# A decoder layer on one core: the first two pairs of heads staged by halves of the tokens beside the projections, and later casts moved from VectorE to GpSimd

## The reference

```
x = layernorm(x + causal_attention(x))            # 16 heads of 16 features, rotary q and k
x = layernorm(x + cross_attention(x, ctx, mask))  # 77 context rows
x = layernorm(x + ffn(x))                         # 256 -> 1024 -> 1024 -> 1024 -> 256, silu gate, gelu, gelu
```

## Time and profile before

| | |
|---|---|
| median of 3 runs | 871.85 us (871.64 to 872.28) |
| the profiled execution's own time | 867.16 us |
| its span in the trace | 865.4 us |
| mean granted clock of TensorE | 0.974 of full speed |
| busy: PE, DVE, ACT, POOL | 803.2, 479.6, 376.2, 321.4 us |

### The profile page before, as it was taken

One profiled execution on the slowest core, in us unless ns is written; L12 is line 12 of the kernel. 1 busy time (PEld: TensorE's weight loads), 2 busy tenths in 40 slices (PEclk: granted clock), 3 DMA queues, 4 the chain that ended last, 5 costly groups with the idle time before them and its releaser, 6 DMA issues.

```text
span 865.4 us, 14094 instructions
## 1 busy us (share of the span) xinstructions
PE 803.2 (93%) x5044; PEld 542.1 (63%) x5044; DVE 479.6 (55%) x1257; ACT 376.2 (43%) x768; POOL 321.4 (37%) x585
## 2 busy tenths in 40 slices
PE   8879988898998999999999888989899899999996
PEld 4544444346776777877777634433577678887886
DVE  3797878536675542155444888871477661125113
ACT  0686776773444211223212377767544432113110
POOL 6313325245312543445332424323631143335433
PEclk9957999999999999999999999999999999999999
DMA  9900534430000232434332035510000000000000
GB/s 274 411 29 33 195 119 147 149 131 1 2 2 25 73 122 74 145 116 141 109 123 73 26 123 182 227 58 2 2 1 2 2 2 1 0 7 20 1 1 26
DMA packets 24712, 68.70 MB, mean 79 GB/s; under 512 B 4449, under 2 KB 11873, under 8 KB 24417
## 3 DMA queue, kind: packets, MB, share of 16 engines
q1 hardware_dynamic: 24640, 67.77, 22.4%
HBM read 65.40 MB, written 13.63 MB: 91 GB/s over the span
## 4 chain that ended last, share of the span: by engine, by line
PE 77%; DVE 10%; ACT 8%; issue 3%; POOL 2%; POOLq 0%; ACTq 0%; DVEq 0%
PE bank_pair L906 27%; PE bank_pair L729 7%; PE bank_pair L894 6%; PE bank_pair L711 6%; ACT prob_s L1048 5%; PE bank_pair L824 4%; PE bank_pair L615 3%; PE bank_pair L761 3%; PE bank_pair L675 3%; DVE bank_pair L1236 3%; PE bank_pair L659 3%; DVE max_raw L1234 3%; PE bank_pair L836 2%; PE bank_pair L903 2%; PE bank_pair L813 2%
## 5 line engine op out<-in xcount | busy, mean ns | idle before, releaser
L1539 POOL TENSOR_TENSOR hid_lo_s<-act_raw_s,hid_hi_s 128x512 fp32r<-128x512 f32 x96 | 124.5, 1298 | 175.4 <-DVE hid_hi_s L1383 136.4
L1048 ACT ACTIVATE prob_s<-bank_pair 128x512 f32<-128x512 f32 (+3 forms) x384 | 163.6, 505 | 57.0 <-PE bank_pair L711 56.5
L1236 DVE CUSTOM_DVE_ANT_0 bank_pair<-bank_pair,causal_bf 128x128 f32<-128x128 f32 (+3 forms) x256 | 120.2, 515 | 43.9 <-PE bank_pair L675 43.5
L675 PE MATMUL bank_pair<-k_t_s,q_t_s 64*128 64x512 f32 (+3 forms) x384 | 120.5, 439 | 3.2 <-DVE max_raw L1234 2.1
L711 PE MATMUL bank_pair<-q_t_s,k_t_s 64*128 64x512 f32 (+3 forms) x384 | 114.5, 409 | 8.4 <-ACT prob_s L1048 4.6
L1500 POOL TENSOR_SCALAR_AFFINE_SELECT prob_s<-prob_s 128x128 f32<-128x128 f32 x256 | 72.0, 295 | 132.1 <-ACT prob_s L1048 129.1
L1383 DVE CAST hid_hi_s<-act_raw_s 128x512 fp32r<-128x512 f32 x64 | 35.9, 565 | 144.8 <-ACT act_raw_s L1115 144.2
L1115 ACT ACTIVATE act_raw_s<-bank_pair,scales 128x512 f32<-128x512 f32 x64 | 42.9, 688 | 160.2 <-PE bank_pair L906 160.2
L711 PEld LDWEIGHTS bank_pair<-q_t_s,k_t_s 64*128 64x128 f32 x384 | 55.7, 190 | 90.5 <-ACT prob_s L1048 69.0
L906 PE MATMUL bank_pair<-hid_hi_s,home_s 128*128 128x512 f32 x256 | 99.8, 390 | 0.8 <-POOL hid_lo_s L1539 0.8
L906 PE MATMUL bank_pair<-hid_lo_s,home_s 128*128 128x512 f32 x256 | 99.6, 389 | 0.0
(11 more groups left out here) (157 smaller groups left out, 1422.3 us busy)
## 6 DMA issues: line engine op xcount, KB each, us to landing
ring_s<-scratch SPq DMA_DIRECT2D x34, 512.0 KB, 3.3
home_s<-scratch SPq DMA_DIRECT2D x22, 512.0 KB, 6.0
checked_s<-in_w_ffn SPq DMA_DIRECT2D x2, 3584.0 KB, 18.2
scratch<-in_w_ffn SPq DMA_DIRECT2D x2, 2560.0 KB, 10.1
ring_moved_s<-scratch SPq DMA_DIRECT2D x10, 512.0 KB, 3.3
checked_s<-in_w_ffn SPq DMA_DIRECT2D x1, 4096.0 KB, 32.4
x_t_s<-in_x_t SPq DMA_DIRECT2D x4, 512.0 KB, 4.2
x_tok_s<-in_x SPq DMA_DIRECT2D x2, 1024.0 KB, 9.1
```

The costliest lines, as they stand in the source:

```text
L675: mm(out[:, 0:k1 - k0], qkt(q, p, 0)[r, P * qt:P * (qt + 1)], qkt(q, p, 1)[r, k0:k1], start=True, stop=True).then_inc(S["max_mm"], 1)
L1048: act.activation(prob[q][4 * (s % 2) + j][:, 0:n], score_bank(s, j)[:, 0:n], ACT.Exp, scale=SCALE).then_inc(S["exp_done"], 1)
L1236: dve.tensor_tensor_reduce(out=out[:, 0:left], in0=out[:, 0:left], in1=L["causal_bf"][:, CHUNK - left:CHUNK], scale=1.0, scalar=NEG, op0=A ...
L1539: pt(dst[1][:, m], act_raw[q][r % 3][:], dst[0][:, m].bitcast(F32), ALU.subtract).then_inc(S["f_lo"], 1)
```

## The change

Sequence 0 alone: the staging, turning and units 0 to 7 of pairs 0 and 1 are done for the first half of the tokens beside the projections (at t = 4 to 11), and the second half of pair 0 is staged and turned there as well (t = 9, 12, 13); pair 1's second half is staged at t = 14. The steps before 0 that remain run from -11 instead of -20. In them run the two last turns of pair 1 (-11, -10), the 16 other units of pair 0 (-11 to -8) and of pair 1 (-7 to -4). The maxima of pair 0 are moved at step -7 instead of -9. The 22 checks of weights are put two to a step into steps -11 to -1. The first 16 units use two banks alternately.

In both sequences: for pairs 2 to 7 the two casts of `stage_hi` are done by GpSimd instead of VectorE, ahead of the two subtractions, which are GpSimd's before and after the change.

```diff
+FIRST_STEP = (-11, pair_base(0) - 13)
+Q_STEP = FIRST_STEP[0] - (NT + V_LAG[0])
+STAGES = [[(Q_STEP + 4, 0, 0), (Q_STEP + 7, 1, 0), (Q_STEP + 9, 0, 1), (Q_STEP + 14, 1, 1)] +
+          [(pair_base(p) - 13, p, None) for p in range(2, NP)], [(pair_base(p) - 13, p, None) for p in range(NP)]]
-def turn_step(p, i):
+def turn_step(q, p, i):
+    if q == 0 and p < 2:
+        return ((Q_STEP + 6, Q_STEP + 6, Q_STEP + 12, Q_STEP + 13), (Q_STEP + 9, Q_STEP + 9, -11, -10))[p][i]
     return pair_base(p) - 12 + i
-def max_step(p, u):
+def max_step(q, p, u):
+    if q == 0 and p < 2:
+        return Q_STEP + 7 + 3 * p + u // 4 if u < 8 else -11 + 4 * p + (u - 8) // 4
     return pair_base(p) - 8 + u // 4
 def check_step(n):
-    return FIRST_STEP + 4 + n * (-FIRST_STEP - 4) // PIECES
+    return FIRST_STEP[0] + n // 2
...
     def unit_bank(q, n):
+        if q == 0 and n < Q_UNITS:
+            return bank[n % 2]
...
         for t in range(NT + V_LAG[0]):
             projections(0, t)
+            attention(0, Q_STEP + t)
...
+        # VectorE: pairs 0 and 1 alone
+        def stage_hi(q, n):
+            step, p, half = STAGES[q][n]
+            t0, t1 = (0, NT) if half is None else (NT // 2 * half, NT // 2 * (half + 1))
...
+        # GpSimd: pairs 2 to 7
+        def stage_hi(q, n):
+            step, p, half = STAGES[q][n]
+            wait(pool, q, "round_mm", ROUND_AT[q][("turn", p - 1, 3)] + 1)
             for i in range(2):
+                src = qk_tok[q][:, i, p].rearrange("p t (h e) -> p (t h) e", h=2).unsqueeze(2).to_broadcast([P, 2 * NT, 2, DH])
+                pool.tensor_copy(stage[q][i][:, :, 0:3 if i else 2:2 if i else 1], src).then_inc(S["stage_hi"], 1)
...
         def attention(q, s):
-            for p in range(1, NP):
-                if stage_step(p) == s:
-                    stage_lo(q, p)
+            for n, (step, p, half) in enumerate(STAGES[q]):
+                if step == s and p >= 2:
+                    stage_hi(q, n)
+                if step == s and n:
+                    stage_lo(q, n)
             if 0 <= s < LAST:
                 select(q, s)
```

More of the change, by code:

```diff
@@ L119, with turns_done @@
 S_END = FINAL_STEP + 1
[L121 to L128, removed]
+ROUNDS = [[], []]
+for _q in range(BATCH):
+    for _s in range(Q_STEP, FINAL_STEP + 1):
+        ROUNDS[_q] += [("turn", p, i) for p in range(NP) for i in range(4) if turn_step(_q, p, i) == _s]
+        ROUNDS[_q] += [("rows", p, 0) for p in range(NP) if rows_step(_q, p) == _s]
+        ROUNDS[_q] += [("y", n, 0) for n in range(2 * NG) if y_step(n) == _s]
+        if _s == 0:
+            EARLY = len(ROUNDS[_q])
+ROUND_AT = [{r: n for n, r in enumerate(rounds)} for rounds in ROUNDS]
+assert ROUNDS[0][EARLY:] == ROUNDS[1][EARLY:]
+def turns_done(q, p, i):
+    return sum(r[0] == "turn" for r in ROUNDS[q][:ROUND_AT[q]["turn", p, i] + 1])
 XG = NG // 2
@@ L138 @@
 X_END = XG * (NT - 1) + X_NORM + 4
[L142 removed]
+LATE_SCORE = 4 * (1 + max(max_step(0, p, u) for p in range(NP) for u in range(NU)))
 BY_VECTOR = [4 * end > LATE_SCORE for end in CHUNK_END]
@@ L179 @@
 FLAG_BANK = 5
-FIRST_UNITS = (2 * NU, sum(max_step(p, u) < 0 for p in range(NP) for u in range(NU)))
+Q_UNITS = 16
+FIRST_UNITS = (2 * NU, sum(max_step(1, p, u) < 0 for p in range(NP) for u in range(NU)))
 SHARED = (6, 2)
@@ L480, in consumer @@
     def consumer(q, n):
-        kind = ROUNDS[n][0]
-        count = sum(r[0] == kind for r in ROUNDS[:n + 1])
+        kind = ROUNDS[q][n][0]
+        count = sum(r[0] == kind for r in ROUNDS[q][:n + 1])
         name = {"turn": "turn_evac", "rows": "rows_evac", "y": "y_norm"}[kind]
@@ L1157, in _ @@
             projections(0, t)
-        for s in range(FIRST_STEP, S_END):
+            attention(0, Q_STEP + t)
+        for s in range(FIRST_STEP[0], S_END):
             attention(0, s)
@@ L1451, in _ @@
         dve.wait_ge(set_pool, 11)
-        for t in range(NT):
-            projections(0, t)
-        for s in range(FIRST_STEP, S_END):
+        for t in range(NT + V_LAG[0]):
+            if t < NT:
+                projections(0, t)
+            attention(0, Q_STEP + t)
+        for s in range(FIRST_STEP[0], S_END):
             attention(0, s)
@@ L1600, in _ @@
         fill(0)
-        for t in range(NT + 1):
-            projections(0, t)
-        for s in range(FIRST_STEP, S_END):
+        for t in range(NT + V_LAG[0]):
+            if t <= NT:
+                projections(0, t)
+            attention(0, Q_STEP + t)
+        for s in range(FIRST_STEP[0], S_END):
             attention(0, s)
```

123 lines of the change are left out of this document (65 added, 58 removed).

## The result

The changed kernel takes 880.64 us (median of 6 runs, 878.02 to 883.44), the kernel before in the same session 871.75 us (866.42 to 873.35). The ratio is 1.0117, 95% interval 1.0086 to 1.0149: slower, by 8.9 us between the medians. The forecast was 876.5, in a range of 870.0 to 882.5. The profiled execution of the changed kernel took 883.35 us, span 881.6. That of the kernel before (867.16) was one of its shorter ones: of its 93 runs in the three later sessions 32 lie at 866 to 868 us and the others at 869 to 877. The two traces therefore stand 16 us apart, more than the kernels do.

The account below looks back on a forecast made before the run. The prediction took TensorE as the bound (busy 93%, 77% of the chain). Late checks, 3.5 us, plus GpSimd's casts, 1.2 us, gave 4.7 us more: the median of 871.85 becomes 876.5 us, range 870.0 to 882.5 (8 in 10).

Parts of the forecast that it names:

- the sum: Whole kernel: 3.5 us from late checks plus 1.2 us from GpSimd's casts, 4.7 us more.
- the second rival: Clock stays low through the projections, or casts cost near their upper bound: +7 to +13 us, chance 17%.
- the full forecast: Projections end at about 43 us, checks late, small cost on GpSimd: +2.5 to +7 us, chance 45%.
- Projections stretched: Opening: work moved beside the projections makes them end at 43.5 us instead of 31.75.
- The schedule at full clock: Projections followed step by step on TensorE without clock loss: last copy ends at 41.5 us, 9.8 us more.
- The lull: TensorE idles before the third unit, waiting for VectorE among the projections: some 2.5 us.
- my bound of 49.5: Latest end of the projections, with the low clock costing 8 us on all remaining tiles and turns.
- Checks behind the last v copy: Opening: ScalarE's 22 checks wait for the last v copy; first exponential 4.0 us later, costing 3.5 us.
- Casts on GpSimd: Stagings of pairs 2 to 7: 0.7 us a cast, 1.2 us in all, from 0 to 10 us.
- The delay of 0.3 us at steps 10 and 22: Masks queued behind GpSimd's staging make the turn wait 0.3 us, four times in two sequences: 1.2 us.
- The sign: Whole kernel: slower by over 0.2%, chance 0.66, resting on the checks coming late.
- No gain from VectorE's relief: VectorE loses 24 casts, 10 us of 480, but is not on the chain there: no gain counted.

Follow-up runs that it names:

- b3: Changed kernel with 24 idle transposes before the third unit and the 22 weight checks spread from step -18 on; ratio 1.0064 to the kernel before.
- a2: Changed kernel with all casts back on VectorE, so the change of the opening alone; ratio 1.0121 to the kernel before.
- a3: Changed kernel whose weight checks read 16 values of each row instead of 1024; ratio 1.0072 to the kernel before.
- b2: Changed kernel with the 22 weight checks spread from step -18 on instead of two a step from -11; ratio 1.0112 to the kernel before.
- b1: Changed kernel with 24 idle transposes, whose result nobody reads, put before the third unit; ratio 1.0054 to the kernel before.
- a1: Kernel before with the casts of pairs 2 to 7 on GpSimd and nothing else; ratio 1.0045 to the kernel before.

## Why the prediction was right, and where its sizes were off

The time lies in the range, but the sum is about half of what was measured: 4.7 us forecast, 8.9 measured. The measured value lies in the span of the second rival (+7 to +13, 17%) and not in that of the full forecast (+2.5 to +7, 45%); the range held because it reached into the rival's.

- **Projections stretched: right, too small.** Two terms were too small. The schedule at full clock was one: I had 17.1 us from the first unit (24.4) to the end of the last copy (41.5), where b3 shows 18.9 to the end of the last v tile and a copy takes 0.4 more. The lull was put at 2.5 us and was 2.89. The clock was the other: I took 2 us, between none and 4, with the end at 43.5. It was 2.5 us in a2, a3 and b2 and 7.0 in the profiled execution, where the clock was low for some 17 of the 23 us from 27 to 50. There the copy ended at 50.24, beyond even my bound of 49.5. That is the rival "clock stays low through the projections". The Trainium skill, "TensorE: Matmul & The Clock Gate", "HAM oscillation — how this bites in real kernels", describes matmuls that fall back to half rate behind a wait; here the trace agrees: the clock went from 1.00 to 0.50 behind a wait of 2.89 us.
- **Checks behind the last v copy: right.** I had 29.7 us from the last v copy's end to the first exponential; the trace has 29.9, and so have a2 (46.52 to 76.41) and b1 (44.73 to 74.62). ScalarE has no idle between the checks that matters, the chain names them, and TensorE waits 0.90 us for the first exponential before its fourth score. Their share of the loss, about 4 us by a3, can be taken away but wasn't won back by an earlier place. The first exponential itself came behind the 71 to 76 us that I had named (80.14, and 76.41 in a2), because the projections ended later than named.
- **Casts on GpSimd: price a little high, no wait seen.** 0.61 us against 0.7 assumed, just below my lower bound of 0.65. The Trainium skill, "GPSIMD Engine Reference", section 3.1, has 768 ns for 512 elements; this measurement is lower. The delay of 0.3 us at steps 10 and 22 didn't come: the casts lengthen a staging by 0.97 us and not by 1.3, and before the change the masks had ended 1.1 us ahead of the products. So no trace shows the 1.2 us of the sum. That the opening alone costs as much as the whole change says the same; a1 is the one number against it, and the ratios are too coarse to tell 1.2 us from nothing.
- **The sum.** 3.5 + 1.2 became 10.9 + 0 in the profiled pair, 7.2 + 0 with a2's opening, and 8.9 between medians. The sign and its mechanism were right.
- **No gain from VectorE's relief: right.** It lost 5.2 us of work, not 10: back to back, a cast holds the queue for 0.34 us (35.89 to 36.23 in the trace before) and not for 0.42, and two of the new half casts took 1.38 us. From the first exponential to the turn of step 22 it is 67.4 us before and 67.5 after.

## What to carry to other kernels

Work that is moved into another stage's queue costs what its waits do to everything behind it in that queue: here some 7.7 us of VectorE's work were hidden at the price of 15 to 18 us on an in-order TensorE (the last copy of v ends at 46.5 to 50.2 us instead of 31.75). Ask of a third engine, even one with no part in the moved work, whether its own load can still fit once its start moves: 28.5 us of ScalarE that had been hidden became the critical path. A lull in a dense stretch of TensorE is to be counted with what the clock does behind it: here 2.89 us of waiting were followed by 2.5 to 7 us lost at half the clock. Whether that costs anything depends on whether TensorE is the bound there. And one trace is one execution: the same opening had its first exponential at 76.41 in one trace and at 80.14 in another.

## What the runs showed of the hardware

- 24 additional transposes, 2.84 us of work in a wait, made the changed kernel 5.5 us faster (1.0117 to 1.0054); in the trace TensorE's granted clock stays at 1.00 for ten microseconds more. A similar filling in the kernel before, where VectorE and ScalarE are nearly full, changed nothing (1.0000).
- A GpSimd cast of 128x512 from float32 to fp32r with a repeated input took 0.61 us, VectorE's 0.42.
- In the changed kernel one of VectorE's half casts took 1.38 us (25.41) while GpSimd added two SBUF tensors (1.26 us from 25.37); later ones of this shape, with no such addition beside them, took 0.28 to 0.29 us (33.42, 48.29). The reductions that end the lull stand behind it in VectorE's queue, so some 1.1 us of the 2.89 are likely due to it; no run without the addition shows it.
